# Top-k experts: from masked products over all tokens to gathered tokens and one-hot sums

## The reference

```
scores   = softmax(norm(x) @ router_w.T)             # over 8 experts
gate, idx = top_k(scores of one expert over the 1024 tokens, 257)   # per batch and expert
h   = gelu(tokens[idx] @ w1[e] + b1[e])              # 128 -> 512
y   = h @ w2[e] + b2[e]                              # 512 -> 128
out = zeros.at[idx].add(y * gate);  x = x + out
```

## Time and profile before

| | |
|---|---|
| median of 3 runs | 1048.47 us (1047.78 to 1049.33) |
| span of the profiled execution | 1043.1 us |
| TensorE busy (products) | 950.8 us, 91% |
| VectorE busy | 743.1 us, 71% |
| ScalarE busy | 691.1 us, 66% |
| GpSimd busy | 219.0 us, 21% |
| HBM read, written | 53.44 MB, 22.94 MB |

### The profile page before, as it was taken

The page is one execution under the profiler, slowest core; times in us unless marked ns, Lnnn a source line. Parts: engine busy times, 40 slices in busy tenths (PEclk is TensorE's granted clock), DMA queues, the critical chain, the costliest instruction groups (busy, mean ns, idle before and its releaser), DMA issues. The chain is left out here.

```text
span 1043.1 us, 16038 instructions
## 1 busy us (share of the span) xinstructions
PE 950.8 (91%) x5690; PEld 617.5 (59%) x5690; DVE 743.1 (71%) x1318; ACT 691.1 (66%) x1180; POOL 219.0 (21%) x494
## 2 busy tenths in 40 slices
PE   3879999999998899999987899999999889999997
PEld 2545555665655677888764344444444367778886
DVE  4786776677644667699875877777777457678996
ACT  2425666666665698888734356666666759898885
POOL 1352355563333000000005113222332200000000
PEclk9999999999999899999999699999999999999999
DMA  3752442213111011355505360111000021115542
GB/s 91 208 174 41 145 115 74 56 63 91 63 42 45 38 41 41 88 136 141 121 3 131 81 184 1 32 32 32 2 2 1 2 81 41 41 62 125 141 150 51
DMA packets 67727, 78.52 MB, mean 75 GB/s; under 512 B 6512, under 2 KB 55552, under 8 KB 67264
## 3 DMA queue, kind: packets, MB, share of 16 engines
q1 hardware_dynamic: 62432, 72.83, 25.2%
q10 hardware_dynamic: 5216, 4.66, 1.6%
HBM read 53.44 MB, written 22.94 MB: 73 GB/s over the span
## 5 line engine op out<-in xcount | busy, mean ns | idle before, releaser
L1062 ACT ACTIVATE b_pt<-b_banks 128x512 f32<-128x512 f32 (+1 forms) x320 | 154.8, 558 | 99.1 <-PE b_banks L976 98.9
L1369 PE MATMUL f_banks<-f_hr,f_w2r 128*128 128x512 f32 x768 | 189.1, 394 | 3.6 <-DVE f_hr L1463 2.5
L1353 PE MATMUL f_banks<-f_xr,f_w1r 128*128 128x512 f32 x768 | 191.4, 397 | 0.7 <-ACT f_h L1437 0.7
L1437 ACT ACTIVATE f_h<-f_banks,b_t 128x512 f32<-128x512 f32 x256 | 167.2, 682 | 32.3 <-PE f_banks L1353 29.8
L1463 DVE TENSOR_TENSOR f_hr<-f_h,f_hr 128x1024 fp32r<-128x1024 f32 x128 | 156.1, 1223 | 28.1 <-ACT f_hr L1443 26.1
L1369 PEld LDWEIGHTS f_banks<-f_hr,f_w2r 128*128 128x128 f32 x768 | 141.7, 188 | 32.3 <-issue 3.4
L1353 PEld LDWEIGHTS f_banks<-f_xr,f_w1r 128*128 128x128 f32 x768 | 143.3, 191 | 29.6 <-ACT f_h L1437 1.5
L1085 DVE TENSOR_REDUCE a_mlate<-a_banks 128x2 f32<-128x1024 f32 (+3 forms) x120 | 124.7, 1079 | 49.8 <-PE a_banks L914 31.1
L1085 DVE TENSOR_REDUCE b_mlate<-b_banks 128x2 f32<-128x1024 f32 (+3 forms) x120 | 125.7, 1080 | 36.1 <-PE b_banks L924 18.0
L1443 ACT ACTIVATE f_hr<-f_h 128x1024 fp32r<-128x1024 f32 x128 | 136.0, 1063 | 4.1
L1062 ACT ACTIVATE a_q_hl<-a_banks 128x512 f32<-128x512 f32 (+1 forms) x160 | 81.8, 557 | 65.0 <-PE a_banks L976 63.5
(11 more groups left out here) (202 smaller groups left out, 1036.5 us busy)
## 6 DMA issues: line engine op xcount, KB each, us to landing
scratch_w<-a_tab SPq DMA_DIRECT2D x16, 512.0 KB, 3.1
f_w1r<-scratch_w SPq DMA_DIRECT2D x16, 512.0 KB, 5.8
f_w2r<-scratch_w SPq DMA_DIRECT2D x16, 512.0 KB, 6.1
v<-scratch_gate SPq DMA_DIRECT2D x32, 256.0 KB, 5.4
xt<-scratch_gate SPq DMA_DIRECT2D x32, 256.0 KB, 5.2
a_rot<-in_w SPq DMA_DIRECT2D x16, 256.0 KB, 4.0
a_q<-scratch_q SPq DMA_DIRECT2D x8, 384.0 KB
a_k<-scratch_k SPq DMA_DIRECT2D x8, 384.0 KB
```

The lines of the kernel that those rows point to most:

```text
L1062: act.activation(pt[at % NPT][:, h, 0:cols], st[u % NST][:, 0:cols], ACT.Exp, scale=scale).then_inc(exp_done, 1)
L1353: last = pe.matmul(h_ps[:, j, :], w1r[e % 2][:, wp, j * P:(j + 1) * P], xr[xp][:, chunk(c)], start=(i == 0), stop=(i == 2))
L1369: last = pe.matmul(y_ps[:, q % 2, :], w2r[e % 2][:, wp, j * P:(j + 1) * P], hr[q % 2][hp][:, j, :], start=(j == 0 and i == 0), stop=(j == ...
L1437: act.activation(h[q % 2][:, j, :], h_ps[:, j, :], ACT.Gelu, bias=m.b1_t[:, e * HB + j:e * HB + j + 1]).then_inc(gelu_done, 1)
```

## The change

The expert stage is rewritten.

- Each (batch, expert) pair is a unit of 257 tokens, padded to 258 columns: two blocks of 128 slots and one "left" token, which is fetched for the 8 experts of a batch together. There are 16 units per layer.
- The normalised rows and the scores are stored to `scratch_rows` (136 floats per token). GpSimd fetches each block of 128 chosen rows by index with an indirect DMA (`fetch`); TensorE turns them (`tokens`).
- The choice is made per batch: the scores are repeated so that each partition holds one expert's 1024 scores, with 16 partitions per expert, each trying another limit. Eight steps (`SHIFTS`), each a count over 1024 columns, find the 257th score. Then ranks, lists of slots and indices are made with small products, ScalarE's Sign and VectorE's sums. Batch 0 is routed ahead of all units; batch 1 is routed in `spot`s between the work of units 0 to 5, all twelve of its later phases on VectorE, with a TensorE product after most.
- y is turned back, multiplied by the gate and split into high and low. The scatter is a product: `hot`, 128 slots x 1024 tokens of zeros and ones in float32r, times y, 2 blocks x 8 token tiles x 2 parts = 32 products of 128 columns into two PSUM banks that hold a batch's sum. `hot` comes from comparing the slot numbers, spread over partitions by SyncE, with the partition's own slot: VectorE compares block 0, GpSimd block 1.
- All 8 experts' weights are held in SBUF (`wr`) and loaded once per layer. SyncE's order: rows, experts 0 and 1, scores, experts 2 to 7, then the placement of batch 0 and its spreads.
- The splits of the tokens before the router are gone. 48 semaphores are shared by the two layers and cleared by GpSimd between them. Two more tables are loaded at the start, with eight VectorE casts or copies.

The core of the diff:

```diff
+SHIFTS = (26, 22, 18, 14, 10, 6, 2, 0)
+UNITS = B * NE
+NXG, NPOS = 6, 3
+PHASES = [(SEARCH, s) for s in range(len(SHIFTS))] + [(COUNTS, 0), (TAKE, 0), (LISTS, 0), (SMALL, 0), (INDEX, 0)]
+VECTOR_AT = {2 * n - 2: PHASES[n] for n in range(1, len(PHASES))}
+TENSOR_AT = {2 * n - 1: PHASES[n] for n in range(1, TOTALS)}
+FIND_AT = {2 * TOTALS - 1: (0, 1), 2 * TOTALS: (2, 3)}
...
     def sync(sp):
+        sp.wait_ge(norm.xn_by_vector, 2 * TPC)
+        store_rows(0)
+        store_rows(1)
+        matrices(0)
...
+        matrices(1)
+        sp.wait_ge(scored, 2)
...
+        for e in range(2, NE):
+            matrices(e)
+        store_place(0)
+        for n in range(UNITS):
+            if n == NE:
+                store_place(1)
+            spread_place(n)
...
+    def gpsimd(pool):
...
+            for i in range(BLK):
+                pool.indirect_dma_start(token[n % NXG][:, i, :], None, m.scratch["rows"],
+                                        by_row(index[b][:, i, e:e + 1])).then_inc(token_in[n % NXG], 16)
+        def one_hot(n):
+            pool.wait_ge(spread_in[n % NPOS], 16 * loads_of_slot(n, NPOS))
+            if n >= 2:
+                pool.wait_ge(added, n - 1)
+            pool.tensor_scalar(hot[n % 2][:, 1, :], spread[n % NPOS][:, :], m.slot[:, 1:2], None, ALU.is_equal).then_inc(hot_by_pool, 1)
+        for n in range(NXG):
+            fetch(n)
+        after = {0: (6,), 1: (7,), 4: (8, 9), **{n: (n + 5,) for n in range(5, UNITS - 5)}}
+        for n in range(UNITS):
+            one_hot(n)
+            for later in after.get(n, ()):
+                fetch(later)
...
     def tensor(pe):
+        def output(n):
+            e = n % NE
+            if n:
+                pe.wait_ge(y_low, n)
...
+            pe.wait_ge(h_low, n + 1)
+            for j in range(HB):
+                for i, (wp, hp) in enumerate(((0, 0), (0, 1), (1, 0))):
+                    last = pe.matmul(y_ps, wr[:, e, 1, wp, j * P:(j + 1) * P], hr[n % 2][hp][:, j, :],
+                                     start=(j == 0 and i == 0), stop=(j == HB - 1 and i == 2))
+        def add(n):
+            pe.wait_ge(hot_ready, n + 1)
+            pe.wait_ge(hot_by_pool, n + 1)
+            pe.wait_ge(y_low, n + 1)
...
+            for i in range(BLK):
+                for t in range(QT):
+                    for part in range(2):
+                        last = pe.matmul(sum_ps[:, t // TPC, t % TPC * P:(t % TPC + 1) * P], hot[n % 2][:, i, t * P:(t + 1) * P],
+                                         yr[n % 2][:, part, i, :], start=(n % NE == 0 and i == 0 and part == 0 and t % TPC == 0),
+                                         stop=False, skip_group_check=True)
...
+        repeat_scores(0)
+        for what, s in PHASES[:TOTALS]:
+            route(0, what, s)
+        for q in range(4):
+            find(0, q)
+        repeat_scores(1)
+        route(1, *PHASES[0])
+        tokens(0)
+        for i in range(UNITS + 2):
             for j in range(HB):
+                if i < UNITS:
+                    hidden(i, j)
+                if j == 1:
+                    if 0 <= i - 2:
+                        turn_back(i - 2)
...
+                    spot(4 * i)
+            if i + 1 < UNITS:
+                tokens(i + 1)
+            spot(4 * i + 1)
+            if 0 <= i - 1 < UNITS:
+                output(i - 1)
+            spot(4 * i + 2)
+            if 0 <= i - 2:
+                add(i - 2)
...
+            spot(4 * i + 3)
...
     def vector(dve):
+        def search(b, s):
...
+                narrow(b, s - 1)
+                link(dve.tensor_tensor(limit[:, :], m.steps[:, 1:2] if s == 1 else ahead[:, :], drop[:, :], ALU.bitwise_or))
...
+            link(dve.tensor_scalar(above_all[:, :], rows[:, :], trial.bitcast(F32), 0.0, ALU.is_ge, ALU.add, accum_out=passed[:, :]))
+            dve.tensor_scalar(enough[:, :], passed[:, :], CAPACITY - 0.5, None, ALU.is_ge).then_inc(count_ready, 1)
...
+        repeat_scores(0)
+        for what, s in PHASES:
+            phase(0, what, s)
+        repeat_scores(1)
+        phase(1, *PHASES[0])
+        left_gates(0)
+        split_tokens(0)
+        for i in range(UNITS + 2):
+            if 0 <= i - 2:
+                one_hot(i - 2)
...
+            spot(4 * i)
+            if 0 <= i - 2:
+                split_output(i - 2)
...
+            spot(4 * i + 1)
+            if i + 1 < UNITS:
+                split_tokens(i + 1)
+            spot(4 * i + 2)
+            if i < UNITS:
+                split_hidden(i)
+            spot(4 * i + 3)
+        finish(1)
```

More of the change, by code:

```diff
@@ L1237, in feed_forward_stage @@
-    h_ps, y_ps = banks[:, 0:HB, :], banks[:, HB:HB + 2, :]
+    many_ready = sem("many_ready")
+    above_all, own = sb("above_all", [P, T], BF16), sb("own", [TE, P])
+    drop, base, ahead, limit = (sb(n, [P, 1], I32) for n in ("drop", "base", "ahead", "limit"))
+    passed, enough = sb("passed", [P, 1]), sb("enough", [P, 1], BF16)
+    above, tied, rank, take_, run = (sb(n, [TE, P]) for n in ("above", "tied", "rank", "take", "run"))
+    count, totals, need, in_tile = sb("count", [TE, 2], BF16), sb("totals", [TE, 2]), sb("need", [TE, 1]), sb("in_tile", [TE, 1], BF16)
@@ L1499, in vector @@
             chunk_norm_vector(dve, m, norm, 3)
-            for c in order:
-                split(c)
         else:
```

724 lines of the change are left out of this document (455 added, 269 removed).

## The result

The changed kernel takes 1075.48 us (median of 4 runs, 1069.92 to 1078.03) against 1048.90 for the kernel before (4 runs, 1047.78 to 1051.75). The ratio is 1.026, 95% interval 1.022 to 1.031: **slower**, where 1043 and "faster" were forecast. The time lies inside the range of 1018 to 1078, between rival 1 (1069) and rival 2 (1093). The profiled execution has a span of 1076.2 us against 1043.1, so 33.1 us are to be found.

A forecast was written before the change was run, and what follows sets the result against it. TensorE, busy 91%, was taken as the bound. Per layer 184.8 us less 1.0 against 187.6 gave 7.6 less for two; start 1.5 and last store 0.5 more left 5.6 less than 1048.5: 1043, range 1018 to 1078.

The forecast's parts named there:

- rival 1: Routing chain longer, ahead of the products and again beside six units: 15% more, 13 us a layer, gives 1069; chance 27%.
- rival 2: Clock stays low beyond the first units or falls again in the sums: 50 us more, 1093; chance 11%.
- Routing of batch 0: Per layer, between score and first product: search, counts, lists and gather exposed with nothing to hide them, 41.3 us.
- its last term: End of batch 0's routing: VectorE's own queue up to the low part of the tokens, hiding the gather, 7.2 us.
- The first six units: Units 0 to 5 of each layer: batch 1's routing phases on VectorE hold up output and sums, together 48.0 us.
- The clock: First units of each layer begin at 1.2 GHz after the routing: 3 us put, with 0 and 12 as ends.
- The steady unit: A unit without routing phases: TensorE needs 7.1 us, with a small wait for VectorE before output 7.7.
- Ten of them: Units 6 to 15 of each layer: ten units at 7.7 us, together 77.
- The closing: End of each layer's stage: two closing rounds of splits, output, sums, left tokens and joins, 15.5 us.
- GpSimd's half: GpSimd's compare of 1024 columns per unit takes 1.0 to 2.5 us, hidden; on VectorE it would cost 1.2.
- Rival 4: GpSimd's half of the compare and VectorE slow each other: at most 5 us a layer, within 1028 to 1058; no separate chance.
- The score 1.0 us earlier: Before the routing in each layer: with the token splits gone, the last logits and score come 1.0 us earlier.

The follow-up runs named there:

- the filled run: Changed kernel with products that nothing reads filling TensorE's waits in the closing and five at the batch boundary: 1063.81 us, ratio 1.015 to the kernel before.
- the bf16 kernel: Changed kernel with one-hot matrices and both parts of the gated outputs written as bf16 instead of fp32r: 1008.66 us, ratio 0.958 to the kernel before.
- the routing filled: Changed kernel with products that nothing reads keeping TensorE busy during batch 0's routing, up to the first unit: 1079.82 us, ratio 1.026 to the kernel before.

## Why the prediction was wrong, step by step

- **Routing of batch 0**, 41.3: right, 42.2 and 41.9. So rival 1 in its first half, a longer chain of dependent steps ahead of the units, did not happen: the whole chain was within 1 us. The search's count took 1.28 us where 1.37 was put. TensorE waited 1.1 us for the last token rows, though three issues in a row take 1.25 us each on GpSimd, near my upper bound of 1.28. The parts of its last term add up to 7.1 and not 7.2.
- **The first six units**, 48.0: this step failed, with 58.4 and 54.6, over the 51.0 with its clock term. By units, forecast 5.3, 6.2, 10.2, 8.4, 8.4, 9.5; layer 0: 7.4, 7.6, 13.2, 9.1, 8.9, 12.2; layer 1: 7.6, 7.5, 11.4, 8.1, 9.2, 10.7. The mechanism was the one I described, phases in VectorE's queue ahead of the split and output and sums behind it; its size was not. Unit 0 missed a table load on ScalarE of 1.28 us and hidden products at 1.2 GHz (2.92 instead of 1.4 us); unit 2 sums at 1.2 GHz (6.92 instead of 3.5); unit 5 sums that are partly at 1.2 GHz (5.30, in layer 0) and two reductions, 2.47 together, ahead of the one-hot half. The run without the second routing prices the phases, clock falls included, at 15.1 and 12.5 us. I had summed VectorE's work, and not asked what the waits that it makes do to the clock.
- **The clock**, 3 us in the first units and nothing after: wrong in size and place. I named its fall in the first units and, as rival 2, in the sums; it fell in both, behind the left sums at the batch boundary and in the closing, but for a few microseconds each time, not for four whole units. The closing lost 4.7 and 3.0 us to it, by the filled run.
- **The steady unit**, 7.7: right to 0.05, with the small wait for VectorE that was named (0.25). **Ten of them**, 77: short by 7.0 and 4.2. The left sums of the first batch, 1.93 us, stand in unit 9 and I had put left sums into the last round only; the wait before output is 0.5 longer there, and most hidden products behind the left sums run at 1.2 GHz (8.99 us for unit 10). In layer 0 another fall stretches unit 6 to 9.1 and these two to 10.65 and 10.1.
- **The closing**, 15.5: 16.7 with the clock held, so 1.2 were missing, and the clock made it 21.4 and 19.7.
- **GpSimd's half**: its 2.9 us lie above my bound of 1.0 to 2.5, taken from a cast and a two-input instruction. VectorE's half took 0.75 and not 1.2. Rival 4 happened as a mechanism (VectorE held up, 8.9 us); against having the half on VectorE it made no difference in time, and what it costs by itself was not measured.
- **The score 1.0 us earlier**: 0.1 in layer 0; in layer 1 the attention was 1.2 longer. The start cost nothing where 1.5 was put; the last store 0.9 instead of 0.5. And the window that began 3.0 us early.

In short: the steps that failed are the 48.0 us of the first six units with the 3 us for the clock, the 77 us of the ten units, which left out the first batch's left sums, and the 15.5 us of the closing with nothing for the clock. The range held in part by luck. Its slower end came from rival 1, 13 us a layer on top of the 89.3 of the routing and the first six units. These took 100.6 and 96.5, 11.3 and 7.2 more, all but 1.5 of it in the rival's second half, the phases beside the units. The other 21 us, of the ten units and the closing, had no place in that rival.

Against the forecast's 1037.5 for the profiled execution (1043.1 - 5.6) the 38.7 us are thus: first six units 7.4 + 3.6, ten units 7.0 + 4.2, closing 5.9 + 4.2, routing 0.9 + 0.6, window 3.0, earlier score 0.9 + 2.2, store 0.4, start -1.5; 38.8 in all.

## What to carry over

When work that was free beside long products is moved in front of and between short ones, price it twice: its own time, and what its waits do to the clock of the engine that waits. A sum of busy times says nothing of that; here waits of 1.4 and 1.8 us stood before a fall that made the next sums 2 us longer. The same two waits brought no fall in the bf16 kernel, so such a term can be given a range but not yet a rule. And when small products with full-size weights make up half of a unit, look at the loads first: two bytes instead of four, or one load for twice the columns, halved their time, which was worth 67 and 42 to 46 us, more than all that the forecast had missed. The first costs precision; the second was tried for its time alone, its output is another one, and a real kernel would have to add up the two parts.

## What the runs showed of the hardware that was not expected

- GpSimd's comparison of 1024 columns takes 2.85 us at the median when it writes fp32r and 2.87 when it writes bf16; VectorE does the same in 0.75 and 0.48.
- An indirect transfer occupies GpSimd for some 0.95 us, and 13 in a row start 1.25 apart, so six units' tokens take 17 us to issue.
- VectorE's instructions grow beside a GpSimd comparison: 0.15 to 1.71 us, a scan from 0.42 to 1.53, a subtraction of 1032 columns from 1.23 to 2.49. The place counts: the one-column L1700 that grows ends 1.14 to 1.15 us behind the comparison's start each time, and a VectorE comparison begun 2.1 to 2.6 us behind it ends 3.4 us behind it; in between, subtractions begun 1.2 to 1.5 us behind the start took their usual 1.23.
- The Trainium skill (SBUF — State Buffer, Who interferes with whom) has VectorE and GpSimd block each other where both read through the shared pair, and calls it an exclusive lock. The growth vanished with the comparisons, which fits; subtractions with two inputs that run beside a comparison at their usual length don't.
- Around unit 1 ScalarE pauses: its second Gelu of that unit starts at 405.02, though the product that it waits for ran from 402.42 to 402.84, and in the kernel without the second routing there is the same pause of 2.28 us. With the routing filled the pauses stood in unit 0. What holds it was not tried and stays open.
